# Attention in a transformer layer: probabilities times values as fp32 matmuls of one head each, softmax by a minimum of negated scores, weighted sums split one turn later

## The reference

```
q, k, v = x_in @ wq.T, x_in @ wk.T, x_in @ wv.T          # four heads of 64
logits = einsum('bhqd,bhkd->bhqk', q, k) / sqrt(64)
logits = where((j <= i) & (j > i - 128), logits, -1e30)
attn = softmax(logits)
out = einsum('bhqk,bhkd->bhqd', attn, v)
out_swa = out @ wo.T
```

## Time and profile before

| | us |
|---|---|
| median of 3 timed runs | 2567.05 (2562.57 to 2570.10) |
| span of the profiled execution | 2562.1 |
| attention phase in it | 0 to 493.2 |
| steady part (turns 8 to 55, 12 groups) | 102.0 to 434.5 |
| turn 56 to the end of the phase | 434.5 to 493.2 |
| TensorE busy in the steady part | 309.5 of 332.5 |
| VectorE / ScalarE / GpSimd busy there | 285.2 / 250.3 / 137.9 |

### The profile page before, as it was taken

How to read it: one execution, slowest core, us unless ns; L and a number is a source line. 1 busy time by engine, 2 the same in 40 slices (tenths; PEclk the granted TensorE clock), 3 DMA queues, 4 the chain that set the end, 5 groups by cost and what they waited for, 6 DMA issues and landing times. The chain is left out here.

```text
span 2562.1 us, 41058 instructions
## 1 busy us (share of the span) xinstructions
PE 2427.1 (95%) x15649; PEld 2156.8 (84%) x15649; DVE 1833.0 (72%) x3835; ACT 1288.7 (50%) x2259; POOL 1343.6 (52%) x810
## 2 busy tenths in 40 slices
PE   6999999799999999999999979999999969999998
PEld 5877887589888889998888867777777759999998
DVE  6888887576777777777676666666666666777766
ACT  3777777644444444444444435565565523444333
POOL 2344344456666666666666633666666643343333
PEclk9999999999999999999999989999999979999999
DMA  3222221340101000000000032322222134444441
GB/s 121 65 87 75 67 81 61 123 170 26 34 26 30 25 26 25 25 26 27 32 30 21 18 120 69 97 95 84 86 82 74 37 123 132 133 137 136 151 141 56
DMA packets 135284, 190.33 MB, mean 74 GB/s; under 512 B 13426, under 2 KB 103959, under 8 KB 134960
## 3 DMA queue, kind: packets, MB, share of 16 engines
q1 hardware_dynamic: 121264, 157.27, 18.9%
q0 software_dynamic: 13824, 30.44, 3.6%
HBM read 123.13 MB, written 72.12 MB: 76 GB/s over the span
## 5 line engine op out<-in xcount | busy, mean ns | idle before, releaser
L690 POOL TENSOR_TENSOR prob<-prob,softmax_small 128x1024 f32<-128x1024 f32 x65 | 124.6, 1917 | 243.4 <-DVE softmax_small L614 243.4
L2112 POOL TENSOR_TENSOR m_hl<-m_hf,m_hh 128x512 fp32r<-128x512 f32 x112 | 168.9, 1521 | 145.7 <-ACT m_hh L1775 145.5
L2473 POOL DMA_INDIRECT out<-e_ys,slot_token x80 | 83.1, 1039 | 231.4 <-DVE e_ys L2429 222.2
L104 PE MATMUL e_ps_y<-r_w_h,e_hl 128*128 128x256 f32 x640 | 181.1, 283 | 0.0
L104 PE MATMUL e_ps_y<-r_w_l,e_hh 128*128 128x256 f32 x640 | 179.0, 280 | 0.0
L104 PE MATMUL e_ps_y<-r_w_h,e_hh 128*128 128x256 f32 x640 | 178.9, 280 | 0.0
L822 POOL DMA_INDIRECT xbuf_d<-xn,scatter_rows x128 | 151.5, 1183 | 47.4 <-issue 38.1
L2362 ACT ACTIVATE e_hf<-e_ps_z,e_b 128x640 f32<-128x640 f32 x128 | 102.0, 797 | 147.1 <-PE e_ps_z L104 140.3
L104 PE MATMUL e_ps_z<-slotsT_h,w_l 128*128 128x320 f32 x512 | 159.1, 311 | 1.3 <-DVE slotsT_l L2407 1.3
L104 PE MATMUL e_ps_z<-slotsT_l,w_h 128*128 128x320 f32 x512 | 159.0, 310 | 0.0
L104 PE MATMUL e_ps_z<-slotsT_h,w_h 128*128 128x320 f32 x512 | 158.8, 310 | 0.0
(11 more groups left out here) (305 smaller groups left out, 9016.1 us busy)
## 6 DMA issues: line engine op xcount, KB each, us to landing
shared_x<-in_x SPq DMA_DIRECT2D x32, 512.0 KB, 5.1
shared_xT<-xT_d SPq DMA_DIRECT2D x64, 256.0 KB, 4.8
new_w1T<-in_W SPq DMA_DIRECT2D x16, 1024.0 KB
new_w2T<-in_W SPq DMA_DIRECT2D x16, 1024.0 KB
xbuf_d<-new_w1T SPq DMA_DIRECT2D x16, 650.0 KB, 8.0
slots<-xbuf_d SPq DMA_DIRECT2D x15, 650.0 KB
xn_d<-xn SPq DMA_DIRECT2D x32, 256.0 KB, 2.5
xT_d<-shared_xT SPq DMA_DIRECT2D x32, 256.0 KB, 2.5
```

The lines of the kernel that those rows point to most:

```text
L104: i = e.matmul(out, a, b, start=first and not onto and n == 0, stop=last and n == len(terms) - 1, skip_group_check=onto)
L690: e.tensor_tensor(p[:], p[:], sm[:, 3].unsqueeze(2).broadcast_to([P, HEADS, 2 * P]), ALU.mult).then_inc(*prob_made(g))
L2112: e.tensor_tensor(hl[:, t, 0:N], hf[(HC * C + t) % NZ][:, 0:N], hh[:, t, 0:N], ALU.subtract).then_inc(*h_low(C, t))
L2473: e.indirect_dma_start(io["out"], bass.IndirectOffsetOnAxis(ap=token[i % 2][:, b:b + 1], axis=0), ys[:, b], None, bounds_check=NT - 1, oob ...
```

## The change

- `attend`: eight plain fp32 matmuls, one head and one block of keys each. The stationary operand is 64 columns of v, the result goes to 64 partitions of PSUM (even heads 0 to 63, odd heads 64 to 127), the moving operand is that head's 128 columns of probabilities. The tile of the array that the built program names for them is 128 rows by 64 columns, at column 0 or 64, where the split matmuls had the whole array.
- Values and transposed probabilities are kept in fp32: `rest_pt` and `rest_v` are gone, `round_pt` and `round_v` become plain copies.
- `round_av` and `rest_av` each become one instruction over 128 partitions, and both are done at turn g+4; ScalarE does `round_av` at the start of the turn.
- ScalarE copies the transposed probabilities after `soft`, not before.
- wq is scaled by -1/8 when it is loaded, so the scores come negated; VectorE takes their minimum, which serves as the bias itself, and the bias instruction is gone. The masks are +1e30.
- `round_x` reads the transposes from PSUM, not from the SBUF copy; the bank is then free when both VectorE and ScalarE have read it.

```diff
-        ps_av = ps("ps_av", [P, KC, 2 * P])
+        ps_av = ps("ps_av", [P, KC, P])
...
-            return {"x": xT_full, "qk": qk_low, "v": v_low, "o": out_full}[kind].at(*key)
+            return {"x": xT_high, "qk": qk_low, "v": v_full, "o": out_full}[kind].at(*key)
...
                 for c2 in range(KC):
-                    vc = slice(c2 * P, (c2 + 1) * P)
-                    i = matmul_split(e, ps_av[:, c2], [(vh[par][:, at + kb, vc], vl[par][:, at + kb, vc]) for kb in range(2)],
-                                     [(pth[g % 2][:, kb, 2 * c2:2 * c2 + 2], ptl[g % 2][:, kb, 2 * c2:2 * c2 + 2])
-                                      for kb in range(2)])
+                    for kb in range(2):
+                        for half in range(2):
+                            h = 2 * c2 + half
+                            i = e.matmul(ps_av[half * DH:(half + 1) * DH, c2], v[par][:, at + kb, h * DH:(h + 1) * DH],
+                                         pt[g % 2][:, kb, h], start=kb == 0, stop=kb == 1)
...
                 for h in range(HEADS):
-                    i = e.activation(p[:, h], p[:, h], ACTF.Exp, bias=sm[:, 1, h:h + 1],
-                                     scale=1.0 / DH ** 0.5, accum_out=sm[:, 2, h:h + 1])
+                    i = e.activation(p[:, h], p[:, h], ACTF.Exp, bias=sm[:, 0, h:h + 1],
+                                     scale=-1.0, accum_out=sm[:, 1, h:h + 1])
...
-                for half in range(2):
-                    r = slice(half * DH, (half + 1) * DH)
-                    i = e.activation(ah[slot(G)][r, :, cols], ps_av[r, :, half * P:(half + 1) * P], ACTF.Copy)
-                i.then_inc(*av_high(g))
+                e.activation(ah[slot(G)][:, :, cols], ps_av[:], ACTF.Copy).then_inc(*av_high(g))
...
             for a in TURNS:
                 early, late = steps_at(a)
+                if a - 4 in turns:
+                    round_av(a - 4)
                 for kind, *key in early:
                     do[kind](*key)
-                if a - 2 in turns:
-                    round_pt(a - 2)
                 if a in turns:
                     soft(a)
-                if a - 3 in turns:
-                    round_av(a - 3)
+                if a - 2 in turns:
+                    copy_pt(a - 2)
...
-                e.tensor_copy(xTh[s][:, :, cols], xT[s][:, :, cols]).then_inc(*xT_high(G, h))
+                e.tensor_copy(xTh[s][:, :, cols], ps_x[:, :, 0:min(2, blocks(G)) * P]).then_inc(*xT_high(G, h))
...
-                        out=p[:, h], in0=ps_s[:, h % 2, h // 2], in1=masks[:, mask], scale=1.0, scalar=-3.0e38,
-                        op0=ALU.add, op1=ALU.max, accum_out=sm[:, 0, h:h + 1])
-                i.then_inc(*top_made(g))
-                dve.wait_ge(*top_made.at(g))
-                e.tensor_scalar(sm[:, 1], sm[:, 0], -1.0 / DH ** 0.5, None, ALU.mult).then_inc(*bias_made(g))
+                        out=p[:, h], in0=ps_s[:, h % 2, h // 2], in1=masks[:, mask], scale=1.0, scalar=3.0e38,
+                        op0=ALU.add, op1=ALU.min, accum_out=sm[:, 0, h:h + 1])
+                i.then_inc(*least_made(g))
...
                 if a - 1 in turns:
                     invert(a - 1)
-                for kind, *key in early:
-                    do[kind](*key)
-                if a - 2 in turns:
-                    rest_pt(a - 2)
-                if a - 3 in turns:
-                    rest_av(a - 3)
-                for kind, *key in late:
-                    do[kind](*key)
+                if a - 4 in turns:
+                    rest_av(a - 4)
+                for kind, *key in early + late:
+                    if kind in do:
+                        do[kind](*key)
```

More of the change, by code:

```diff
@@ L251, in attention_phase @@
         w2Th, w2Tl = shared.w2T()
[L252 to L257, removed]
+        v = [sb(f"values{i}", [P, 9, D]) for i in range(2)]
+        small = [sb(f"softmax_small{i}", [P, 3, HEADS]) for i in range(NPR)]
+        pt = [sb(f"probT{i}", [P, 2, HEADS, P]) for i in range(2)]
         ah = [sb(f"attnT_h{i}", [P, KC, GRP * P], F32R) for i in range(2)]
@@ L294, in attention_phase @@
         xT_high = signal("xT_high", kinds["x"])
-        qk_low, v_low = signal("qk_low", kinds["qk"]), signal("v_low", kinds["v"])
-        top_made, bias_made, recip_made, pt_low, av_low = (
-            signal(n, turns) for n in ("top_made", "bias_made", "recip_made", "pt_low", "av_low"))
+        qk_low = signal("qk_low", kinds["qk"])
+        least_made, recip_made, av_low = (signal(n, turns) for n in ("least_made", "recip_made", "av_low"))
         xT_full = signal("xT_full", kinds["x"])
-        qk_high, v_high = signal("qk_high", kinds["qk"]), signal("v_high", kinds["v"])
-        exp_made, pt_high, av_high = (signal(n, turns) for n in ("exp_made", "pt_high", "av_high"))
+        qk_high, v_full = signal("qk_high", kinds["qk"]), signal("v_full", kinds["v"])
+        exp_made, pt_full, av_high = (signal(n, turns) for n in ("exp_made", "pt_full", "av_high"))
         out_full, w1_high, w2T_high = signal("out_full", kinds["o"]), signal("w1_high", range(4)), signal("w2T_high", range(2))
@@ L320, in v_dst @@
             if G == MEM:
-                return [(vh[b][:, 0:1], vl[b][:, 0:1]) for b in range(2)]
+                return [v[b][:, 0:1] for b in range(2)]
             at = 1 + (G % 2) * GRP + 2 * h
-            return [(vh[G // 2 % 2][:, at:at + 2], vl[G // 2 % 2][:, at:at + 2])]
+            return [v[G // 2 % 2][:, at:at + 2]]
         def qk_dst(G, t):
@@ L473, in round_v @@
                     act.wait_ge(*av_done.at(8 * (G // 2 - 2) + 7))
-                for high, _ in v_dst(G, h):
-                    i = e.activation(high, ps_v[:, 0:min(2, blocks(G))], ACTF.Copy)
-                i.then_inc(*v_high(G, h))
+                for full in v_dst(G, h):
+                    i = e.activation(full, ps_v[:, 0:min(2, blocks(G))], ACTF.Copy)
+                i.then_inc(*v_full(G, h))
             def copy_out(G, m):
@@ L588, in rest_qk, with least @@
                 i.then_inc(*qk_low(G, t))
-            def rest_v(G, h):
-                ps_v = bank("v", G, h)[:].rearrange("p (j d) -> p j d", j=2)
-                dve.wait_ge(*v_high.at(G, h))
-                for high, low in v_dst(G, h):
-                    i = e.tensor_tensor(low, ps_v[:, 0:min(2, blocks(G))], high, ALU.subtract)
-                i.then_inc(*v_low(G, h))
-            def maxima(g):
+            def least(g):
                 p, sm, mask = pr[g % NPR], small[g % NPR], place(g)[2]
@@ L622, in rest_av @@
                 dve.wait_ge(*av_high.at(g))
-                for half in range(2):
-                    r = slice(half * DH, (half + 1) * DH)
-                    i = e.tensor_tensor(al[slot(G)][r, :, cols], ps_av[r, :, half * P:(half + 1) * P],
-                                        ah[slot(G)][r, :, cols], ALU.subtract)
-                i.then_inc(*av_low(g))
+                e.tensor_tensor(al[slot(G)][:, :, cols], ps_av[:], ah[slot(G)][:, :, cols], ALU.subtract).then_inc(*av_low(g))
             def rest_w2T(k):
@@ L2561, in window_masks @@
     q, k = np.arange(P)[:, None], np.arange(P)[None]
-    masks = np.full((3, P, 2 * P), -1e30, np.float32)
+    masks = np.full((3, P, 2 * P), 1e30, np.float32)
     masks[0, :, :P][k > q] = 0
@@ L2565, in window_masks @@
     masks[1] = masks[0]
-    masks[1, :, :P - NMEM] = -1e30
+    masks[1, :, :P - NMEM] = 1e30
     masks[2, :, :P][(k >= P - NMEM) & (k <= q)] = 0
```

41 lines of the change are left out of this document (20 added, 21 removed).

## The result

The changed kernel takes 2542.22 us (median of 4 runs, 2542.12 to 2542.76) against 2567.98 us (4 runs, 2562.57 to 2570.10) beside it: a ratio of 0.9905, with a 95% interval from 0.9893 to 0.9917. That is 25.8 us less; 2551 was forecast. By the profiled executions the span goes from 2562.1 to 2541.0 us, 21.1 less. The median of before stands 5.9 above its profiled span, the new one 1.2, so the medians differ by more than the spans: the runs of before lie up to 7.5 apart, and its profiled execution is near their lower end. For places within the kernel I compare spans and starts; where two kernels are compared as a whole I say which figures are used.

What follows compares the result with a forecast made beforehand. TensorE was taken to set the pace, VectorE close behind. Steady part 11.2 us less, turns ahead 1.5, turns 56 to 63 1.0, drain 1.5: together 15.2, so 2551 us; own range 2541 to 2560, full range 2538 to 2598.

Steps and rivals of the forecast that it cites:

- The likeliest case: Whole kernel: the column halves overlap in attend, making it faster; overlap given 0.60, faster 0.55, predicted time 2551 us.
- Attend, 1.29 us: Attend matmuls on TensorE: 0.99 us of overlapped passes plus 0.30 for the array's shape change, 0.17 less than before.
- only the second pass of one head can run beside the first of the next: Attend matmuls: claimed limit on overlap of the column halves, giving 9 steps, 0.99 us.
- Second x half: Second half of the x transposes on TensorE: its wait of 0.92 us for VectorE's rest of v goes.
- Waits that stay and come: TensorE's waits per group: 0.5 at q projection, 0.45 at j=0, 0.95 at j=2; 1.9 against 2.15 us.
- Turns 56 to 63: Turns without q/k/v projections: 4.4 us each, 5.9 with an output projection; 35.3 against 36.3, 1.0 less.
- Ends: Nine turns ahead of the steady part 1.5 us less; the drain behind the last turns 1.5 less.
- VectorE's relief: Some 9 us of VectorE's 24 a group saved; claimed worth nothing by itself, paying only in waits.
- The rival in sequence: Attend: fp32 passes on the two column halves do not overlap; 29 us slower, 2596; chance 0.26.
- partly overlapping: Attend takes 11 to 13 steps, or new waits eat the gain; 2560 to 2567, no change; partial overlap 0.11.
- Tiles work independently: Skill's rule for attend's array tiles: gives 1.3 us a turn; without it 2.1.
- weight loads overlap running matmuls only where the row group differs: Skill's rule behind the attend rival of exposed weight loads: some 80 us slower, 2649; chance 0.03.

Runs made afterwards that it cites:

- E1: Changed kernel with attend's eight matmuls issued all on one column half first, then all on the other; 2566.43 us, ratio 0.9991.
- E5: E3 with GpSimd's two x rests moved ahead of its multiplication of the probabilities; 2517.32 us, ratio 0.9798.
- E3: Changed kernel with the sums split in attend's own turn again and the probabilities copied ahead of the exponentials; 2528.11 us, ratio 0.9843.
- E6: E3 with attend as four plain fp32 matmuls on the whole array, two heads each, and sums split in two instructions per engine; 2556.98 us.
- E2: Changed kernel with sums split in their own turn, probabilities copied ahead of the exponentials, and x rounded from the SBUF copy; 2532.06 us, ratio 0.9858.
- E4: Changed kernel with VectorE's low half of the sums' split put ahead of the minima, not behind them; 2546.14 us, ratio 0.991.

## Why the prediction was right, and where it was short

The forecast was 2551 us and faster, its own range 2541 to 2560, and 2542 came. The likeliest case is the one that happened; two terms of its sum were too small, for the waits of the steady part and for turns 56 to 63. That the total came near owes something to luck: by the profiled spans these two brought 11 us more than forecast, the ends and the later phases 5.1 us less, and 2542 is only 1 us inside the lower end of its own range.

- **Attend, 1.29 us.** Measured 1.30. Its two parts were each a little off and cancel: the overlap is complete, 8 steps (0.88) and not 9, since rows of the two halves start together; and what is left of it is 0.42 and not 0.30: 0.17 on entering, 0.10 on leaving, and 0.15 within (1.03 - 0.88), of which 0.05 is each half's first step (0.16) and the rest lies behind the last pass. The step "only the second pass of one head can run beside the first of the next" was wrong; E1 shows why: each half has its own stream, and it starts even ahead of program order.
- **Second x half.** Its wait of 0.92 is gone, as said.
- **Waits that stay and come: 1.9 a group forecast, 1.3 measured.** This is the mis-sized term. The places are those named; the sizes are 0.62 for x (0.5 forecast), 0.14 at j=0 (0.45), 0.55 at j=2 (0.95). At j=0 the split was expected at s+3.1, s being the start of the scores. It starts at 339.43 and is done for attend at 339.88, s+2.95; and TensorE comes by at s+2.80 and not s+2.67, since the shape change falls ahead of attend and not behind it. At j=2 it is the same: ready at s+3.9 and not at s+4.15. The gain from waits is 2.15 - 1.3 = 0.8 a group where I had 0.25, and the group is 26.1 us against the 26.8 forecast: -19.5 for the twelve, not -11.2. Attend and waits make 1.5 of the 1.6 a group; I have not located the rest.
- **Turns 56 to 63.** 3.96 us and 5.56 where 4.4 and 5.9 were forecast: -3.7 in place of -1.0, though 1.2 of it is the lower clock of before in turn 62. The chain is the one I named (minima, reciprocal, split, attend). Attend starts at s+2.93 (450.28 - 447.35) and not s+3.1, and the next scores 1.03 behind it and not 1.29: the 0.17 of entering passes while attend waits, and the 0.10 of leaving lies in the scores' own time.
- **Ends.** The nine turns gave 1.9 where I forecast 1.5, but the first scores started 1.75 later, for which the sum had no term; the scaling of wq cost nothing, as said. Of the 3.6 us by which E5 starts turn 8 ahead of E3, 2.0 are GpSimd's order, which I had not looked at. The drain lost 1.2 where I forecast 1.5 less. I had taken its saving from the shorter splits and walked no chain there, nor did I give the clock a term. TensorE stops for 2.35 and 1.02 us for splits of sums, but before it stopped for the same, and no shorter (2.70 ahead of the last attend, 1.75 ahead of the output projection), and kept its upper level; now its clock is at the lower one from the last attends on. What made it fall here and not there these runs do not show.
- **VectorE's relief "is worth nothing by itself, TensorE being the pace; it pays only in waits".** Right here, and under-priced. In E6 it carries a longer attend and wins 12 us all the same. How much of the gain of the change is TensorE's and how much VectorE's can be read in a group: 0.16 x 4 = 0.64 from attend, 0.8 from waits.
- **The range and the sides.** The rival in sequence, to which I gave 0.26 and the upper end, did not occur. With the halves half overlapped (E1) the kernel is at 2566, no change, as was given for "partly overlapping" (2560 to 2567).
- **The rules weighed.** Tiles work independently (the Trainium skill, TensorEngine Tiling (Array Packing), Key Properties): the 16 rows in 1.09 us agree. That weight loads overlap running matmuls only where the row group differs (the Trainium skill, TensorE: Matmul & The Clock Gate, What overlaps and what doesn't) does not hold here either: the two halves have the same rows, and loads of 137 ns do not show in steps of 0.11. The same passage says that matmuls start and end strictly in order; the row starts of E1, read as two streams, disagree.
- **What the forecast had no term for.** That the later split is itself a loss of 14 us. I priced its waits (1.4 a group) and did not ask what the kernel would do without it. By medians the change is the sum of a gain of 40 us (E3) and a loss of 14; by spans, of 35 and 14.

**Open.** The phases behind the attention take 1.1 us longer, while their instructions are the same. In the nine profiles of this case they take from 2065.7 us (E1) to 2067.5 (the changed kernel), so the 1.1 is no larger than what the executions differ by; I do not read it as an effect of the change. What set the clock in the drain and in the opening is open. E2 and E3 differ in x alone, but the split of the probabilities was not brought back alone, so its own share is not shown. The fully sequential attend stays unmeasured; the nearest to it is E6.

## What to carry to other kernels

Work that is taken off a near-critical engine should not be spent on moving its remaining waits elsewhere: a wait on an engine with slack (VectorE's 116 us for ScalarE in E3) is free, and the same microsecond on the engine that sets the pace, or ahead of it in the order of a queue, is not. When a change has several parts, price each order by where the last wait of each turn ends, in the turns with little work too: those decided E3 and E4. And after a change that frees an engine, look at the waits that are left and at who could serve them first; here two lines on GpSimd (E5) were worth 11 us more.

## What the runs showed of the hardware

- **Column halves are independent streams.** Two fp32 matmuls on 64 columns of the array each, with 128 columns flowing, advance together at 0.11 us a pass (16 rows in 1.09 us), and a half that is free is served while three or four passes of the other, which stand ahead of it in the program, have not started (E1).
- **A pass costs by the columns that flow, but one column costs as much as 128.** An fp32 pass takes 0.11 us for 128 columns, and in E6 0.215 for 256 (in windows of 0.02 us its rows start from 342.12 to 343.42 at that pace); E6's rows last 379 ns against 273. One column cost 0.11, as much as 128; between them nothing was measured.
- **Weight loads of half the columns are shorter**: a load of 128 rows by 64 columns lasts 137 ns against 190 for E6's of 128, and is hidden behind the running pass in both (minimum/median/maximum in ns, loads and matmuls, the change's, then E6's):

```profile
L423 PEld LDWEIGHTS ps_av<-probT,values x64: 132/137/137, 339.9 to 359.7; 128*64 128x64 f32 x64
L423 PE MATMUL ps_av<-probT,values x64: 272/273/323, 339.9 to 359.9; 128*64 128x128 f32 x64
```

```profile
L421 PEld LDWEIGHTS ps_av<-probT,values x56: 190/190/192, 301.7 to 343.2; 128*128 128x128 f32 x56
L421 PE MATMUL ps_av<-probT,values x56: 379/379/382, 301.8 to 343.4; 128*128 128x256 f32 x56
```

- **A cast from SBUF beside GpSimd waits for it, one from PSUM does not.** The same rounding of x (minimum/median/maximum in ns), before from SBUF and after from PSUM:

```profile
L581 DVE CAST w_h<-shared_xT x22: 394/1258/2122, 106.3 to 383.3; 128x512 fp32r<-128x512 f32 x22
```

```profile
L577 DVE CAST w_h<-ps_proj x24: 677/679/682, 104.6 to 392.6; 128x512 fp32r<-128x512 f32 x24
```

From SBUF the slow one of a pair takes about as long as GpSimd's multiplication of 1.9 that runs then; from PSUM all take 0.68. Undisturbed, the one from SBUF is the shorter (0.39). E2 has the SBUF form again, with 395/1257/2121. The Trainium skill (SBUF — State Buffer, SBUF: two separate sides) describes the ports that VectorE and GpSimd share as an exclusive lock for the whole instruction, and these rows agree.
